# Two changes of order in a graph kernel: TensorE's root product between two bias products, and VectorE's weights ahead of the mask

## What is computed

```python
# layer 0: pooled messages, maximum over the edges of a node
m   = x[src] * (1 + softplus(coeff) * w[:, None])
p   = relu(layer_norm(m @ pool_w + pool_b, g_p, b_p))
agg = maximum(segment_max(p, dst), 0)
h   = relu(layer_norm(concat([x, agg]) @ final_w + final_b, g_f, b_f))
x   = norm(x + h)
# layer 1: relational layer with 8 bases, mean over the edges of a node
msg = [segment_sum(x[src] * comp[type][:, b:b+1], dst) / max(deg, 1) for b in range(8)]
y   = concat([*msg, x]) @ weight.reshape(-1, 128) + bias
out = norm(x + y)
```

## Time and profile before

| what | us |
|---|---|
| median of 3 runs | 863.32 |
| lowest and highest of them | 862.43, 863.52 |
| the profiled execution | 862.27 |
| its span, first to last instruction | 860.5 |
| fill, up to the first root-side transposes | 0 to 27.7 |
| dense steps | up to 462 |
| the steps 101, 102, 103 on PE | from 464.8, 472.7, 477.8 to 483.9 |
| edge steps from 104 | 484.9 to 605 |
| stage C | 608 to 860.5 |

### The profile page before, as it was taken

One profiled execution on the slowest core, in us unless ns is written; L12 is line 12 of the kernel. 1 busy time (PEld: TensorE's weight loads), 2 busy tenths in 40 slices (PEclk: granted clock), 3 DMA queues, 4 the chain that ended last, 5 costly groups with the idle time before them and its releaser, 6 DMA issues.

```text
span 860.5 us, 17875 instructions
## 1 busy us (share of the span) xinstructions
PE 767.1 (89%) x4519; PEld 542.2 (63%) x4519; DVE 756.1 (88%) x2605; ACT 593.2 (69%) x2887; POOL 692.1 (80%) x801
## 2 busy tenths in 40 slices
PE   5799999999999999999999999998399999988950
PEld 4577777777777777777777787776244444444430
DVE  6999999999999999999998999986288999999960
ACT  4699999999999999999999988886001111211130
POOL 2699999999998999999996677777677777777777
PEclk9799999999999999999999999998599999999985
DMA  4367777767777767767766444353288877889811
GB/s 111 116 222 230 227 232 246 232 222 230 223 222 232 230 217 229 237 215 228 230 220 196 147 121 123 115 171 134 91 301 281 290 285 289 295 287 300 288 48 45
DMA packets 90699, 179.84 MB, mean 209 GB/s; under 512 B 17161, under 2 KB 36018, under 8 KB 84326
## 3 DMA queue, kind: packets, MB, share of 16 engines
q1 hardware_dynamic: 73414, 147.26, 49.3%
q0 software_dynamic: 15744, 30.96, 14.6%
q10 hardware_dynamic: 1440, 0.50, 0.4%
HBM read 109.02 MB, written 70.91 MB: 209 GB/s over the span
## 4 chain that ended last, share of the span: by engine, by line
DVE 31%; POOL 23%; ACT 22%; issue 11%; PE 10%; DMA 2%; DVEq 0%; SPq 0%; ACTq 0%; POOLq 0%
POOL out_rows L431 11%; POOL rows L438 10%; ACT junk L779 9%; DVE work L1185 7%; ACT work L819 5%; DVE bn L1121 5%; DVE work L1133 4%; DVE outb L1196 4%; ACT xT L841 3%; PE ps L569 2%; PE ps L598 2%; ACT junk L831 2%; PE ps L601 2%; ACT st L796 2%; DVE agg_all L1167 2%
## 5 line engine op out<-in xcount | busy, mean ns | idle before, releaser
L779 ACT ACTIVATE junk<-ps 128x128 bf16<-128x128 f32 x884 | 227.7, 280 | 11.7 <-PE ps L601 9.1
L779 ACT ACTIVATION_READ_ACCUMULATOR junk<-ps 128x1 f32 x884 | 189.4, 214 | 0.0
L731 PE MATMUL ps<-agg_all,w_cen 128*128 128x512 f32 (+1 forms) x400 | 176.9, 596 | 7.2 <-DVE agg_all L1280 6.6
L569 PEld LDWEIGHTS ps<-w_cen,work 128*128 128x128 f32 x984 | 122.8, 196 | 47.7 <-issue 46.9
L598 PE MATMUL ps<-w_cen,xT 128*128 128x128 f32 x984 | 150.8, 286 | 0.6 <-ACT xT L841 0.6
L569 PE MATMUL ps<-w_cen,work 128*128 128x128 f32 x984 | 146.8, 294 | 0.0
L1280 DVE TENSOR_TENSOR agg_all<-coefs,ps 128x1024 f32<-128x1024 f32 x98 | 117.5, 1208 | 32.5 <-PE ps L717 19.7
L472 POOL TENSOR_TENSOR work<-work,vec_raw 128x512 f32<-128x512 f32 x98 | 124.6, 1271 | 22.3 <-DVE work L1185 19.5
L598 PEld LDWEIGHTS ps<-w_cen,xT 128*128 128x128 f32 x984 | 131.4, 199 | 7.4 <-issue 5.5
L731 PEld LDWEIGHTS ps<-agg_all,w_cen 128*128 128x128 f32 x400 | 75.4, 194 | 92.7 <-issue 92.1
L1121 DVE BATCH_NORM_STATS2 bn<-work 128x6 f32<-128x128 f32 x492 | 126.1, 277 | 3.6 <-DVE work L1133 0.9
(11 more groups left out here) (147 smaller groups left out, 1409.2 us busy)
## 6 DMA issues: line engine op xcount, KB each, us to landing
coefs<-coef_line SPq DMA_DIRECT2D x49, 1024.0 KB
rows<-in_x SPq DMA_DIRECT2D x97, 256.0 KB
x_table<-work SPq DMA_DIRECT2D x97, 256.0 KB
out_rows<-outb SPq DMA_DIRECT2D x97, 256.0 KB
x_dst_table<-x_dst SPq DMA_DIRECT2D x98, 64.0 KB
rows<-x_dst_table SPq DMA_DIRECT2D x24, 256.0 KB
apart<-apart_line SPq DMA_DIRECT2D x14, 224.0 KB
x_dst<-in_x,dst_i POOLq DMA_INDIRECT x98, 3.3
```

The lines of the kernel that those rows point to most:

```text
L569: last = pe.matmul(Y[b][:, cols(m, m + 1)], x1T[:, b, m, :], w_cen[:, W_ROOT, :], start=False, stop=True, skip_group_check=True)
L731: last = pe.matmul(MT[b][:, 0:n * D], w_cen[:, W_BASE + m, :], prod[:, b, m, 0:n, :].rearrange("p t d -> p (t d)"), start=(m == 0), stop=( ...
L779: last = nc.scalar.activation(junk[:, kind * CH + m, :], bank[:, cols(m, m + 1)], ACT.Square, accum_out=power[:, b, 1, TOP + kind * CH + m ...
```

## The change

It touches the order of calls in two places, and nothing else. On PE, steps 101 to 103 keep the call list of the dense steps but for one pair: `rooted` is called ahead of `first_bias`. In the diff the new first branch (c < DENSE + 3 = 101) is the old list, and the `elif` is the list with the pair exchanged, for c = 101, 102, 103. On DVE, behind step 0, `bottom_and_root` runs ahead of `mask`. Every instruction and every wait is the one it was.

```diff
-                if c < EDGE_ORDER:
+                if c < DENSE + 3:
                     turned()
                     root_bias()
                     first_bias()
                     rooted()
+                    first_layer()
+                    rows_turned()
+                    pooled_turned()
+                    pooled_layer()
+                elif c < EDGE_ORDER:
+                    turned()
+                    root_bias()
+                    rooted()
+                    first_bias()
                     first_layer()
                     rows_turned()
                     pooled_turned()
...
             def early():
+                bottom_and_root()
                 mask()
-                bottom_and_root()
```

## The result

| what | before, us | after, us |
|---|---|---|
| median of 5 runs each | 863.32 | 859.92 |
| lowest and highest | 862.22, 863.52 | 858.33, 860.55 |
| ratio of the two, 95% interval | | 0.9968 [0.9955, 0.9982] |
| the profiled execution | 862.27 | 858.33 |
| its span | 860.5 | 856.5 |

The kernel is faster by 0.32%, 3.40 us by the medians and 4.0 by the two spans. In the new kernel the lines behind PE's new branch are 9 further down: L1109 of before is L1118 here, L1133 is L1142, L779 is L788, L841 is L850, L990 is L999.

What follows compares the result with a forecast made beforehand. ACT was taken to pace the dense steps, PE to bound the edge steps, DVE to make the fill's path. Terms 1.29 + 1.0 + 0.47 = 2.76 us took the median from 863.32 to 860.56; range 858.8 to 862.8.

Steps and rivals of the forecast that it cites:

- the full sum: All terms at full size, fall of PE's clock and wait both gone: 1.29 + 1.79 + 0.47 = 3.55 us.
- The fill, 1.29: VectorE's step 0: weights run inside the wait for `d_prev`, step-2 variance goes from 14.14 to 12.85, gaining 1.29 us.
- lower bound of 0.7: Fill: the gain in us if the load of `rest_in` landed 0.6 us after 8.9.
- Step 101, 1.0 between 0.18 and 1.79: PE's root product fills the wait before L590: 0.18 us with full clock throughout, at most 1.79, taken as 1.0.
- Steps 102 and 103, 0 + 0.47: PE's new order: nothing in step 102, set by ACT; 0.47 us in step 103, where ACT's squares wait.
- worth nothing: Step 102: ACT's work hides the exchange; without that cover it would be worth up to 1.1 us.
- under 0.1 a step: Price of PE's new weight-loading order, in us, hidden in steps 101 to 103 behind the residual or ACT.
- case C: Median runs have the clock's fall; it and the wait go: 3.55 us, 859.77, or 858.7 if like the profiled execution; chance 0.12.
- The forecast of 2.76: Whole kernel: summed gain in us of fill 1.29, step 101 1.0 and step 103 0.47.
- B: Most executions of the kernel before have no clock fall in step 101: gain 1.94 us, 861.38; chance 0.25.
- D: Fill gives nothing, another load or PE's low clock holding the dense steps' start: 861.85, or 862.7; chance 0.14.
- E: Edge steps: shifted waits make TensorE's clock fall, 1.6 us each; slower from three more falls, 865.4; chance 0.07.

## Why the prediction came out right

**Predicted 860.56, measured 859.92.** The sign and the path were as forecast, and the main rows that the new profile was to show are there. The sum came close in part by luck, as the terms show one by one.

- The weights start at 8.77 (said: near 8.9) and L1017, the old L1008, at 26.22 (near 26.1).
- The clock holds, and ACT has no marked wait before the squares of H in steps 101 and 103.
- L580 of step 104 is at 480.90 (near 481.3 with the full sum).
- The first scatter is at 474.04 (474 to 476) and the last at 601.32 (near 602).
- The advance behind step 103 arrived whole: POOL's one dependence on these steps was passed on, as argued from the earlier trace rows.

**The fill, 1.29: right for this pair of profiles, half as large on average.** It measured 1.15, and 1.23 at step 101. The path was right. That the size was right too is partly luck. The next to be late was `edge_beta`, at 12.51, not ACT's squares (12.47 + 0.22 = 12.69). I had both within 0.15 us of each other, so the value held (12.98 against 12.85). In the seven profiles with the new order `edge_beta` was the later one three times and ACT's squares four times. The mis-sized part is the other end. I took the old kernel's 14.14 as given ("the profiled execution has both landings"), and that execution had the latest landing of the mask's load of the five with the old order: 11.19, where the others had 10.15 to 10.85. The term that hung on a landing should have had the range of the landings, which one trace can't give. My lower bound of 0.7 stood for another load and not for this one, and single pairs go down to 0.1.

**Step 101, 1.0 between 0.18 and 1.79: the clock's part right, the other mis-sized.** No profile has a step worth 1.0, which was the middle between two cases. Without the fall it is worth 0.59, and with it 0.59 + 1.63 = 2.22, which is beyond my upper bound. For the fall I had worked out 3.3 x 0.49 = 1.6; it measured 1.63. For the end without a fall I took ACT's idle time as the profile names it, corrected for the clock, 0.18. It measured 0.59. What I had missed is that ACT loses more than the wait that is marked: the second wait, of 0.22, bore no mark, and the first one cost 0.12 beyond its mark. The trace of before could have said so. Its timeline of ACT in step 101, around the row of 471.64 in the earlier trace rows:

```profile
469.63 0.22 ACT L779 ACTIVATION_READ_ACCUMULATOR junk<-ps 128x1 f32 x1
...
472.57 0.22 ACT L779 ACTIVATION_READ_ACCUMULATOR junk<-ps 128x1 f32 x1
472.88 0.28 ACT L831 ACTIVATE junk<-ps 128x128 bf16<-128x128 f32 x1
```

The distances between the starts give 471.64 - 469.63 - 0.09 = 1.92 and 472.88 - 472.57 - 0.09 = 0.22, together 2.14. That is near the 2.22, where the mark alone gave 1.79.

**Steps 102 and 103, 0 + 0.47: 0.54 measured together.** The size was right, the working only in part. That PE would come too early in step 102 after the advance of step 101, and that the root product covers it, came true: with the old order there it waits 0.75. But the exchange in step 102 is not "worth nothing" because ACT's work hides the wait. Without it ACT's squares start 0.40 and 0.21 late, and the wait of step 103, to which I had given the 0.47, is not there. The two steps were not tried apart. And the price of the order, "under 0.1 a step" and hidden, measured 0.25 to 0.30 and is not hidden: step 102 takes 5.37 us instead of 5.12. My sum had nothing for it. The order is worth 1.13 with this price already taken off.

**Sum.** Without the fall my terms make 1.94 for the profiled execution and the measured ones 1.15 + 1.13 = 2.28. With it they make 3.55 against 3.91, where the spans show 4.0. The two profiled executions are thus a pair of the case C of the rivals, which I had given 0.12. The forecast of 2.76 lay between C and B, and the median gain of 3.40 is nearer to C. The likely ways to it are that the clock fell in most of the timed executions of before, or that the fill's gain was above its average there. Which of them it was, no run tells: the first chip has no run of a half.

**The rivals.** B (no fall in most executions) lives on: the fall is missing in two of four profiles. The Trainium skill, "TensorE: Matmul & The Clock Gate", Part 1, cited in the prediction, says of the rise at a kernel's start that its place is run-variable for the same kernel. The traces agree in kind, for a fall: here the same kernel took 16.18, 17.82 and 16.19 us in the same stretch. D (the fill gives nothing) is refuted in the profiles: the dense steps start earlier, and step 101 with them. E (clock falls in the edge steps) is refuted for the first chip. The same steps, 4 us earlier, have the same clock of 0.99 as the earlier trace rows and the same busy time:

```profile
481.00:596.00 115.00, 109.58 (x767) 0.99 0.44 138
```

A window cut at the old times would have shown 0.97, because the low clock at the stage's end has moved into it. When a stage moves, its window has to move too.

## What to carry to other kernels

Where an engine waits at the head of its queue and has work in the same step that does not need the awaited result, exchanging the two can be worth more than the wait that the consumer behind it is marked with (here 0.59 us against ACT's 0.27). Count it by the distance between the starts of the consumer's instructions, take off what the new order itself costs (here 0.25 to 0.30 us a step), ask whether the wait comes back in the next step, and keep what the clock may add as a separate term that some executions have and others don't. Where the wait is for a transfer, the time of landing is a range and not a number, and so is the gain. Before moving a small VectorE operation away from a GpSimd one that stretches it, see which operation will stand in its place.

## What the runs showed of the hardware

- **One wait, two outcomes.** A PE wait of 1.00 us was followed by the lower clock level in two of four profiles (granted 0.51 and 0.55 over some 3.3 us, a cost of 1.63 us) and by no fall in the other two, nor behind six waits of 0.98 to 1.05 in the steps from 104 on.
- **A second place of the same kind.** From L554 at the end of the fill to L554 of step 101 it is 437.03 to 437.13 us in nine profiles. In three others (437.73, 437.91, 438.91) the granted clock was 0.50 or 0.51 from 42 to 46 us, where the nine had 0.57 to 1.00, and the product near 60 us (L554 or the L563 behind it) came 0.6 to 1.0 us later. Two had 437.98 and 438.07 without that, and of the 1.8 us of the profile with 438.91 this explains 1.0 at most. Such a difference is as large as the fill's gain, and hides it in single runs. The profile with 438.91, the fill alone:

```profile
42.00:46.00 4.00, 3.81 (x15) 0.51 0.65 218
```

- **The order of products.** In PE's steps with the root product ahead of the bias, the same products took 3.77 or 3.78 us, with it behind the bias 3.48 to 3.53.
- **Landings.** Behind an unchanged queue, VectorE's mask began with the landing of `d_prev` at 10.15 to 11.73 us in the eight profiles where it waited for it.
- **Small operations beside GpSimd.** A 3x128 copy takes 0.99 instead of 0.21 us and a 128x4 operation 0.94 instead of 0.15 when GpSimd's 1.26 us addition runs beside it.
- **Chips differ.** Two other chips ran this kernel 10% slower. Their profiles have waits of several microseconds from 480 us on (6.76 on ACT and 7.13 on PE in the rows above), for which the profile names no engine of the core. The cause is open.
